# A fused two-layer perceiver block on one core: paired tiles and a host-transposed context in the first cross attention, the context's normalisation on ScalarE in the second, norms by chunks of four tiles, weights loaded a stage earlier

## The reference, cut to what matters

```python
x = x + _L0_xattn_ref(_layernorm(x), ctx_1024, ctx_1024, mask, Wq, bq, Wk, bk, Wv, bv, Wo, bo)   # 16 heads of 8
x = x + _L0_attn_ref(_layernorm(x), ...)          # gated delta rule
x = x + _L0_ffn_ref(_layernorm(x), ...)           # 8 experts, top 2
x = x + _L1_xattn_ref(ctx_1024, _layernorm(x), Wq, Wkv, Wout, gm, bm, gl, bl)   # 8 heads of 64
x = x + _L1_attn_ref(_layernorm(x), ...)
x = x + _L1_ffn_ref(_layernorm(x), ...)           # causal attention over 32, then 8 experts

# _L0_xattn_ref                                   # _L1_xattn_ref(x=ctx, latents)
qh = heads(q @ Wq.T + bq)                         xn = layernorm(x, gm, bm)
kh = heads(k @ Wk.T + bk)                         ln = layernorm(latents, gl, bl)
vh = heads(v @ Wv.T + bv)                         q = ln @ Wq
attn = where(valid, qh @ kh * scale, -inf)        k, v = split(concatenate([xn, ln]) @ Wkv)
out = softmax(attn) @ vh                          out = softmax(q/scale @ k - max) @ v
return out @ Wo.T + bo                            return out @ Wout
```

## Time and profile before

| | |
|---|---|
| median of 3 runs | 3080.18 us (3079.72 to 3081.09) |
| the profiled execution's own time, its span | 3079.37 us, 3077.6 us |
| granted TensorE clock, mean of the span | 0.962 of full |
| busy: PE, PEld, DVE, ACT, POOL | 2819.4, 1618.6, 1978.6, 1479.6, 1906.0 us |
| mean of one: GpSimd's addition L444; its gain L1646, shift L1656, addition L1686 | 2.37; 1.96, 1.94, 1.27 us |
| mean of one: VectorE's residue L590 of 512 columns; 13 aggregates L1860 together | 0.75; 0.95 us |
| second loop, the step around 2000 us: TensorE starts `scores(b+1, 0)` | 1997.39 |

### The profile page before, as it was taken

How to read it: one execution, slowest core, us unless ns; L and a number is a source line. 1 busy time by engine, 2 the same in 40 slices (tenths; PEclk the granted TensorE clock), 3 DMA queues, 4 the chain that set the end, 5 groups by cost and what they waited for, 6 DMA issues and landing times. The chain is left out here.

```text
span 3077.6 us, 66754 instructions
## 1 busy us (share of the span) xinstructions
PE 2819.4 (92%) x22718; PEld 1618.6 (53%) x22765; DVE 1978.6 (64%) x4504; ACT 1479.6 (48%) x2385; POOL 1906.0 (62%) x1278
## 2 busy tenths in 40 slices
PE   5799999999999978998899999999999997888789
PEld 2355555555555566775344444444444443777356
DVE  5477777777777744114667767767767744776653
ACT  3466666666666522333544444444444434223633
POOL 5487878787878721001488888888888872553500
PEclk8899999999999989998999999999999998999789
DMA  7655555555555210001000000000000000000300
GB/s 184 187 174 193 177 190 181 184 186 179 194 175 188 100 58 1 1 0 39 22 33 21 21 32 21 21 32 21 21 32 21 21 1 9 3 3 2 85 5 10
DMA packets 146463, 233.18 MB, mean 76 GB/s; under 512 B 16787, under 2 KB 85851, under 8 KB 146076
## 3 DMA queue, kind: packets, MB, share of 16 engines
q1 hardware_dynamic: 145180, 228.87, 22.7%
q10 hardware_dynamic: 1152, 2.49, 0.6%
HBM read 147.80 MB, written 83.52 MB: 75 GB/s over the span
## 5 line engine op out<-in xcount | busy, mean ns | idle before, releaser
L444 POOL TENSOR_TENSOR sb_a_acc<-sb_a_acc,sb_a_PT 128x1024 f32<-128x1024 f32 x252 | 596.7, 2368 | 36.6 <-ACT sb_a_PT L522 30.3
L522 ACT ACTIVATE sb_a_PT<-ps_a_SC 128x1024 f32<-128x1024 f32 (+1 forms) x416 | 425.8, 1023 | 315.3 <-PE ps_a_SC L794 291.7
L607 DVE TENSOR_REDUCE sb_a_mx<-ps_a_A 128x1 f32<-128x512 f32 x768 | 506.4, 685 | 97.0 <-PE ps_a_A L771 91.8
L1686 POOL TENSOR_TENSOR sb_a_acc<-sb_a_acc,sb_a_PT 128x512 f32<-128x512 f32 (+2 forms) x384 | 487.5, 1269 | 37.3 <-ACT sb_a_PT L1782 10.9
L1782 ACT ACTIVATE sb_a_PT<-ps_a_SC 128x1024 f32<-128x1024 f32 (+2 forms) x256 | 234.3, 915 | 563.0 <-PE ps_a_SC L2061 329.3
L1875 DVE TENSOR_REDUCE sb_a_mx<-ps_a_A 128x1 f32<-128x512 f32 x384 | 256.5, 679 | 280.1 <-PE ps_a_A L2036 240.1
L2080 PE MATMUL ps_a_PV<-sb_a_PT,sb_a_XN 128*128 128x512 f32 (+2 forms) x896 | 434.3, 601 | 2.2 <-ACT sb_a_PT L1782 0.7
L2061 PE MATMUL ps_a_SC<-sb_a_QX,sb_a_XT 128*128 128x512 f32 (+1 forms) x832 | 396.7, 596 | 0.1
L771 PE MATMUL ps_a_A<-sb_a_KS,sb_a_QS 97*128 97x512 bf16 x768 | 301.9, 394 | 30.6 <-issue 17.7
L794 PE MATMUL ps_a_SC<-sb_a_QS,sb_a_KS 105*128 105x128 bf16 (+1 forms) x3328 | 257.3, 220 | 13.4 <-DVE sb_a_QS L621 13.4
L805 PE MATMUL ps_a_PV<-sb_a_PT,sb_a_V 128*32 128x256 f32 (+1 forms) x3328 | 266.7, 392 | 0.4 <-issue 0.3
(11 more groups left out here) (516 smaller groups left out, 5265.3 us busy)
## 6 DMA issues: line engine op xcount, KB each, us to landing
sb_a_C<-in_ctx_dram SPq DMA_DIRECT2D x64, 768.0 KB
a_KD<-sb_a_K SPq DMA_DIRECT2D x192, 256.0 KB, 4.1
sb_a_KS<-a_KD SPq DMA_DIRECT2D x256, 192.0 KB
a_KD<-sb_a_K SPq DMA_DIRECT2D x192, 144.2 KB, 2.7
sb_a_KS<-a_KD SPq DMA_DIRECT2D x256, 108.2 KB
sb_a_QP<-a_QD ACTq DMA_DIRECT2D x6, 384.0 KB, 14.7
sb_a_up<-in_moe_up_dram SPq DMA_DIRECT2D x1, 2048.0 KB, 7.9
sb_a_dn<-in_moe_dn_dram SPq DMA_DIRECT2D x1, 2048.0 KB, 12.0
```

The source lines that it names most:

```text
L444: pool.tensor_tensor(acc[:, :], first[:, :], PT[slot(a, j)][:, :], ALU.add).then_inc(s["acc"], 1)
L522: act.activation(PT[slot(a, j)][0:n, :], SC[(a + j) % 2][0:n, :], ACT.Exp).then_inc(s["exp"], 1)
L607: v.tensor_reduce(mx[:, p, c:c + 1], A[u % 2][:, :], AXX, ALU.max).then_inc(s["am"], 1)
L1686: pool.tensor_tensor(acc[a][0:m, :], first, PT[u % 4][0:m, HQ * i:HQ * i + HQ], ALU.add).then_inc(s["acc"], 1)
```

## The change

1. **`xattn0`.** The host transposes the context (`ctx_T`) and the four weights. `load` brings one transposed batch straight into `CT` (820 KB in one DMA); the 13 transposes and 4 copies per batch are gone, and the weights' four transposes and copy in the prologue. The step goes by pairs of tiles, with even numbers of maxima. GpSimd adds seven tiles in place of nine, TensorE takes two more by ones. Keys of chunks 0 and 1 are made half a step earlier (for b+3 in step b). SP spills and stacks group by group and loads b+4 last; in the prologue the load of batch 2 stands behind the stacks of batch 0.
2. **Norms.** Statistics, power and scaling by chunks of four tiles (four powers of 128x4). In `moe0`, `xattn1` and the second norm of `ffn1` TensorE's following matmuls start between the chunks.
3. **`xattn1`.** Weights transposed on the host and loaded during `delta0`, seven more DMAs on SP's queue there. The context is normalised by ScalarE (13 activations with a scale and a bias per row): chunk 0 of b+3 at the end of unit 7 of step b, chunks 1 to 3 of b+2 in units 1, 3 and 5. VectorE gives a second 128x13 tensor_scalar in exchange (-mean), GpSimd a product of 128x13. `moments` moves from unit 4 to between `top` and `topped`.
4. **`ffn1`.** One array of host-prepared weights, loaded by one DMA in `delta1`; its transposes, copies and permutations are gone.

```diff
-    COUNT = (0, 2, 2, 2, 2, 3, 3, 3, 3, 3, 3, 0, 0)
+    NG = (NK + 1) // 2
+    COUNT = (3, 5, 5, 5, 5, 3, 0)
+    SUMS = (1, 2, 4, 5, 7, 8, 9)
...
             def load(b, a):
-                wait(sp, s["ct"], 4 * (b - 1))
-                sp.dma_start(C[a][:, :, :], d["ctx_1024"]...)
-                sp.dma_start(CR[a][:, :], d["ctx_1024"]...)
+                wait(sp, s["vp"], 4 * (b - 1))
+                sp.dma_start(CT[a][:, :], d["ctx_T"][dsl(b), :, :].rearrange("o d s -> d (o s)")).then_inc(s[f"ld{a}"], 16)
             def step(b, a, n2, n4):
-                if n4:
-                    load(b + 4, a)
                 if n2:
                     for g in range(2):
                         spill(b + 2, a, g)
-                    for g in range(2):
                         stack(b + 2, a, g)
+                if n4:
+                    load(b + 4, a)
...
             def step(b, a, n1, n2, n3):          # TensorE
+                for g in range(NG):
+                    us = list(units(g)) if n1 else []
+                    if g == 0 and n2:
+                        keys(b + 2, a, 2)
+                    if g + 1 < NG:
+                        for j in pair(g + 1):
+                            if g > 0:
+                                maxima(1)
+                            scores(b, a, j)
+                        maxima(1)
+                    if g == 1 and n2:
+                        keys(b + 2, a, 3)
+                    if g == 2 and n2:
+                        values(b + 2, a, 0)
+                    if g in (4, 5) and n3:
+                        keys(b + 3, 1 - a, g - 4)
+                    if g > 0:
+                        maxima(1)
+                    if g == NG - 1 and n1:
+                        top(b + 1)
+                    for j in pair(g):
+                        products(b, a, j)
+                    maxima(len(us))
...
                 total(b)
                 if n2:
                     values(b + 2, a, 3)
+                if n1:
+                    for j in pair(0):
+                        scores(b + 1, 1 - a, j)
...
             def step(b, a, n1, n2, n3):          # VectorE
                 if old:
                     emptied(b - 1)
+                if n2:
+                    residue(b + 2, 2)
+                for g in range(NG):
+                    for i, u in enumerate(units(g) if n1 else ()):
+                        tops(b + 1, u)
+                        if i == 3 and g == 1 and n2:
+                            residue(b + 2, 3)
+                        if i == 3 and g == 4 and n3:
+                            residue(b + 3, 0)
                 if n1:
                     top(b + 1)
+                if n3:
+                    residue(b + 3, 1)
+                if n1:
                     topped(b + 1, 1 - a)
...
     moments(0)                                   # norm_vector
     moments(1)
     scaled(0)
     moments(2)
     scaled(1)
     moments(3)
     if meanwhile is not None:
         meanwhile()
     scaled(2)
     scaled(3)
...
+            def normed(b, a, c):                 # xattn1, ScalarE
+                wait(act, s["nb"], b + 1)
+                for j in range(4 * c, min(4 * c + 4, NK)):
+                    m = wcols(j)
+                    act.activation(C[a][0:m, j, :], C[a][0:m, j, :], ACT.Identity, bias=nb[a][0:m, j:j + 1], scale=crs[a][0:m, j:j + 1])
...
                     if two and u == 7:
                         queries(b + 2, a)
                         latents(b + 2, a)
+                    if three and u == 7:
+                        normed(b + 3, 1 - a, 0)
...
-                    if u == 4 and three:         # xattn1, VectorE
-                        moments(b + 3, 1 - a)
                 if one:
-                    top(b + 1, 1 - a)
+                    top(b + 1)
                 if three:
-                    norm(b + 3, 1 - a)
+                    moments(b + 3, 1 - a)
+                if one:
+                    topped(b + 1, 1 - a)
```

More of the change, by code:

```diff
@@ L197, in norm_vector, with scaled @@
+    def scaled(c):
+        v.wait_ge(s["rstd"], c + 1)
+        for n in range(4 * c, 4 * c + 4):
+            v.tensor_scalar(dst[:, n, :], src[:, n, :], k.mv[:, n, 0:1], k.rstd[:, n:n + 1], ALU.subtract, ALU.mult)\
+             .then_inc(s["norm"], 1)
+    moments(0)
+    moments(1)
+    scaled(0)
+    moments(2)
+    scaled(1)
+    moments(3)
     if meanwhile is not None:
         meanwhile()
[L199 to L202, removed]
+    scaled(2)
@@ L553, in _ @@
             for c in range(4):
-                turned(1, 1, c)
-            for c in range(4):
                 keys(1, 1, c)
@@ L561, in _ @@
                 values(1, 1, c)
-            for c in range(4):
-                turned(2, 0, c)
             act.wait_ge(s["qw"], 96)
             spread(act, *SPANS[1], s["ldq1"])
-            probs(0, 0, 0)
+            for j in pair(0):
+                probs(0, 0, j)
             values(1, 1, 3)
+            for c in range(2):
+                keys(2, 0, c)
+                second(2, 0, c)
             step(0, 0, True, True, True)
@@ L780, in top @@
                 wait(pe, s["m1"], b + 1)
[L781 to L784 removed]
+                pe.transpose(A[0][:, 0:P], mxm[:, :], k.ident[:, :]).then_inc(s["mt"], 1)
             def scores(b, a, j):
@@ L860, in _ @@
             for c in range(4):
-                turn(1, 1, c)
-            for c in range(4):
                 keys(1, 1, c)
@@ L865, in _ @@
                 values(1, 1, c)
-            for c in range(4):
-                turn(2, 0, c)
             pe.wait_ge(s["qc"], NT // 4)
@@ L873, in _ @@
             top(0)
-            scores(0, 0, 0)
+            for j in pair(0):
+                scores(0, 0, j)
             values(1, 1, 3)
+            for c in range(2):
+                keys(2, 0, c)
             step(0, 0, True, True, True)
@@ L1782, in probs, with step @@
                 act.activation(PT[u % 4][0:m, 0:n], SC[u % 2][0:m, 0:n], ACT.Exp).then_inc(s["exp"], 1)
-            def step(b, a, pair, one, two):
+            def step(b, a, pair, one, two, three):
                 for u in range(NB):
@@ L1810, in _ @@
             heads_in(0)
+            for c in range(4):
+                normed(0, 0, c)
             turned_queries(0, 0)
@@ L1951, in _ @@
                 moments(b, b)
-            for b in range(2):
-                norm(b, b)
             for u in range(NU):
                 tops(0, u)
-            top(0, 0)
+            top(0)
+            topped(0, 0)
             step(0, 0, 0, True, True)
```

463 lines of the change are left out of this document (213 added, 250 removed).

## The result

The changed kernel takes 3172.14 us in the median of four runs (3168.3 to 3175.46), the kernel before 3080.43 in the same comparison: a ratio of 1.0297, with a 95% interval of 1.0279 to 1.0315. It is 92 us slower, where 19 us faster was forecast and 3090 was the range's upper end. The profiled execution has a span of 3171.1 us.

What follows compares the result with a forecast made beforehand. TensorE, busy 95 to 97% in two loops holding 1916 of 3077.6 us, was taken as the bound. Terms -11+2-4-4-2-7.5-6.5+22-8 = -19 gave 3061 us, range 3015 to 3090.

Steps and rivals of the forecast that it cites:

- the first loop's part: First cross attention's loop: -0.4 us per step, -11 over 29 steps (-46 to +9), SP's new order priced at nothing.
- would come back if it did: First loop: the wait for a stack at the first maxima returns if SP's path ends a wait; no size given.
- My own sign of being wrong: Wrong if the wait at turn is absent, or the first loop's step is under 29.5 or over 31.5 us.
- TensorE's part of the first loop: First loop, per step: -2.8 us of work and idle places, against 2.4 of waits on the maxima's reduces.
- The second loop: xattn1's loop: moments' move saves 0.7 us per step, the wait at turn costs 1.5; +22 in all (-20 to +70).
- Rival D: Second loop: moments delays topped, two tensor_scalars at 1.042 us each, aggregates 0.95; +36 us, 3097; chance 0.04.
- The starts: Block starts, weights loaded early: second cross attention -7.5 us (-5 to -10), last block -8 (-6 to -9.5).
- Steps 0 and 1: Second cross attention's first two steps: VectorE's normalisation of two batches and a 4.0 us wait gone, -6.5 us (-3 to -9).
- The norms: Norms in chunks let TensorE start earlier: moe0 -4 us, the last norm -4, delta0 -2.
- A: Second loop: the wait at turn does not arise as ScalarE's stream shifts forward; -20 for +22, 3019 us; chance 0.20.
- B: First loop: VectorE paces the paired maxima, +0.3 us per step; +9 for -11, 3081, no change; chance 0.16.
- C: Second loop: the wait at turn is dearer, slower from 2.4 us per step, 3109 at 3.2; chance 0.14.

Runs made afterwards that it cites:

- e1_order: Changed kernel with SP in a first-loop step issuing both spills, then both stacks, then the load: 3049.38 us, ratio 0.9894 to the kernel before.
- e4: Changed kernel with setup and first cross attention of the kernel before put back, all else as changed: 3092.69 us, ratio 1.0035.
- v5: Kernel of e1_order, ScalarE's four normalisations ahead of its query and latent copies, batches 0 and 1 normalised by VectorE in xattn1's prologue: 3002.14 us, ratio 0.9746.
- e2: Changed kernel with the load of batch b+4 issued by ScalarE at its step's end, SP's order as changed: 3079.56 us, ratio 0.9994.
- v2: Kernel of e1_order, all 13 tiles normalised by VectorE behind topped, moments left between top and topped, GpSimd's product left out: 3391.25 us, ratio 1.1001.

## Why the prediction was wrong

*The step that failed* is the last sentences of the first loop's part: SP "orders spill, stack, spill, stack; this path did not end a wait in the step, so I price it at nothing". That a path ends no wait before says how it stood in the old order. What the runs show in its place is a wait for landings of 12 us per step and steps of 34.0 us instead of 30.84, and `e1_order` takes 123 us back by that order alone. My own sign of being wrong, a step over 31.5, was met. The trace of the kernel before had what it takes to walk the new order: two spills of six DMAs, their landings of 4.1 and 2.7 us, two stacks of eight DMAs in 5.8 us each. In the old order both spills wait on keys, not on each other's landing; in the new one SP stands still for each landing in turn and the second spill is behind the first stack. A sum of the new queue gives 3.8 + 4.1 + 5.8 + 2.8 + 2.7 + 5.8 + 0.4 = 25.4 us with the old landings, most of a step before any wait for keys. That is still 5 us under a step, so it would have made a rival of this path and not yet the forecast; with the landings as they became it is 33.4, and that they would grow no row showed. The half sentence "would come back if it did" named the symptom and gave it neither a price nor a chance.

*TensorE's part of the first loop* was right in direction and too small in size: 29.83 us without the queue's cycle against the 30.84 that I forecast. I had charged 2.4 us for waits on the maxima's reduces; the row shows 0.55. The floor of 28.4 (31.24 - 2.8) was right: TensorE is busy 28.5 us per step in `e1_order`. The new step as a whole is worth 1.4 us (e4 gives 43 for the stage), not 0.4; how much of it the pairs are is not shown.

*The clock* was not in my sum. The slow step shown holds 4.0 us of idle time (0.29, 1.48 and 2.26), the good one 1.7 (0.30, 1.19 and 0.21); that is 2.3 of the 5.9 us between them. The other 3.6 is the busy time of the same 327 matmuls, 32.26 and 28.66, at a granted clock of 0.86 and 1.00. The clock is 1.00 until 449, while TensorE waits 0.29 and 1.48 us, and 0.50, the lower of its two levels (1.2 GHz), from 450 to 460:

```profile
446.00:449.00 3.00, 1.23 (x17) 0.80 (x14) 0.47 (x1) 0.67 (x1) 2.43 (x2) 1.00 0.38 117
450.00:460.00 10.00, 7.74 (x56) 3.94 (x48) 5.50 (x9) 5.18 (x7) 5.99 (x4) 0.50 0.42 116
```

So it fell ahead of the wait of 2.26 us, and a maximum takes 0.61 at 450.42 where it took 0.39 at 448.83. Over the whole loop, 29 steps each and the same matmuls, the changed kernel and `e1_order` compare so:

```profile
134.29:1120.91 986.62, 876.95 (x9367) 524.20 (x9370) 671.26 (x1126) 533.60 (x752) 590.56 (x346) 0.94 0.51 169
134.07:998.94 864.87, 825.40 (x9367) 499.52 (x9370) 670.47 (x1125) 530.02 (x752) 589.09 (x346) 1.00 0.59 193
```

Of the 121.8 us between them 51.6 are busy time, at a clock of 0.94 and 1.00, and 70.2 are idle time. The clock took more than the idle time in the pair of steps above, and less in the loop.

*The second loop* came as forecast: a wait of 1.55 to 1.66 per step against 1.5, +25.9 us against +22. The price of a tile was 0.385, where I had interpolated 0.34. The estimate from the Trainium skill, "ScalarE: Activation LUTs", section "What ACT_TABLE_LOAD costs", 0.386, is what the trace shows.

*Rival D* was mis-sized in both its terms: the two tensor_scalars take 0.17 each (2083.05 and 2083.13), not 1.04, while GpSimd stands idle there (2079.29 to 2083.38), and the 13 aggregates 2.76 in place of 0.95, which no run explains. Together 3.1 us as summed, by luck. `topped` is in time by little: its first result is written at 2083.92, and the scores that need it start at 2084.50.

*The starts*: weights loaded early gave nearly what the last block's rows promised (-6.9 against -8; the first queries come 5.7 us earlier in their block), and 5 less than forecast in the second cross attention, because ScalarE's normalisation in the prologue stands in the queries' way; v5 gives 9.5 of it back. Steps 0 and 1 gave -2.3 against -6.5, but -5.9 in `e1_order`, whose block is the same; the 3.6 us between these two have no cause on record. Ahead of the first loop I had +2 (the load's 820 KB at 180 GB/s are 4.6 us, not about 4); TensorE's wait for the keys of batch 1 is 9.2 us there in place of 17.2, because it starts later, and the loop opens 0.9 us earlier. The traffic at the start of `delta0` is no 3% either (DMA share 0.72 in the first 11 us of its norm); the early loads cost nothing there even so, as TensorE's first wait is 6.54 us against 6.42.

*The norms* were summed at -10 and gave about 1. Each norm's first transposes start earlier, as forecast. In `moe0` the last transposes, on which the router waits, move little: they end 12.7 us behind the first statistics, where it was 12.2. In `delta0` TensorE's first matmuls behind the norm start 0.4 us earlier, but 32 of them take 6.82 us at a granted clock of 0.50 where they took 5.03 at 0.70, and the next group 6.39 against 5.45. The +2.1 of the table is therefore the clock's and not the chunks': in e4 and e2, with the same chunks, `delta0` takes 83.6 and 84.0 us. What decides between these clocks is not shown.

*Rivals* A, B and C didn't occur. None of my rivals was the one that happened, and the slower side of the range rested on the second loop alone.

## What to carry to other kernels

When a change reorders a queue that issues DMAs, add up the new queue as a cycle: issue, landing, what stands behind it on the same queue, back to the first; a slack in the old order proves nothing. An idle engine's releaser is one link: follow it until the wait that has no waiting ahead of it, since here the row named VectorE and the cause was SP's order. And where two engines share access to the same memory, an instruction that moves later can collide with the other engine's stream and cost several times its own length.

## What the runs showed of the hardware

VectorE's tensor_scalar of 128x128 from and to SBUF takes 0.33 us in the median of the kernel before. In v2, started while GpSimd works, nine take 14.66 us, 1.6 each, and in the mean of all 205, with those that find GpSimd still, 1.36. Reduces from PSUM are not touched (0.675 in the same run, 0.679 before). The Trainium skill, "SBUF — State Buffer", section "Who interferes with whom", describes the port shared by these two engines as an exclusive lock for a whole instruction; the rows agree with it. GpSimd's power takes 1.02 us for 4 columns, 2.44 for 13 and 2.90 for 16, so four small ones are dearer than one. The larger spill (256 KB) lands in 4.1 us in the median of the kernel before, 6.3 in the changed one, 3.7 in e2 and 7.7 in e1, with the same 233.2 MB moved by each; the fastest loop of the four is the one with the longest landing, since nothing in it stands still for one. TensorE's granted clock was 0.50 for about 10 us of the slow step, and 0.94 in the mean of the changed loop against 1.00 in `e1_order`'s, which has 70 us less idle time.
